# A 12,500-node graph network with a routed feed-forward stage: one of 32 row gathers of layer one becomes 128 one-row transfers

## The reference

```
def gcn_layer(x, W, b):                       # used twice
    support = x @ W
    msgs = support[src] * edge_weight[:, None]
    return segment_sum(msgs, dst, 12500) + b

h = elu(gcn_layer(layernorm(x), W1, b1))
h = elu(gcn_layer(h, W2, b2))
x = x + h
xf = layernorm(x)
H = gelu(xf @ ffn_W1 + ffn_b1)                # hidden 1024
probs = softmax(H @ Wg + bg)                  # 8 experts
e = argmax(probs)                             # one expert per node
x = x + probs[e] * (H @ Wd[e] + bd[e])
```

## Time and profile before

| | |
|---|---|
| median of 3 runs | 6100.4 us (6088.14 to 6104.39) |
| profiled execution | 6100.27 us |
| its span | 6098.5 us |
| mean granted TensorE clock | 0.746 of full speed |
| PE busy | 3582.9 us (59%) |
| PEld busy | 3351.2 us (55%) |
| POOL busy | 3256.1 us (53%) |
| DVE busy | 2006.6 us (33%) |
| ACT busy | 1122.0 us (18%) |
| DMA engines, software queue q0 (the gathers) | 27.9% of 16 engines' span |
| DMA engines, hardware queue q1 | 6.0% |

### The profile page before, as it was taken

One profiled execution on the slowest core, in us unless ns is written; L12 is line 12 of the kernel. 1 busy time (PEld: TensorE's weight loads), 2 busy tenths in 40 slices (PEclk: granted clock), 3 DMA queues, 4 the chain that ended last, 5 costly groups with the idle time before them and its releaser, 6 DMA issues.

```text
span 6098.5 us, 84880 instructions
## 1 busy us (share of the span) xinstructions
PE 3582.9 (59%) x21458; PEld 3351.2 (55%) x21459; DVE 2006.6 (33%) x6596; ACT 1122.0 (18%) x1692; POOL 3256.1 (53%) x3403
## 2 busy tenths in 40 slices
PE   2455555455555545466556556555656555566999
PEld 2454445444544445465555555555556555565888
DVE  6222222222222222233333333333333333336333
ACT  3111111111111111032222222222222222221111
POOL 5566666566666666545555445545555554542444
PEclk6666666666666666677777777777777777778999
DMA  7333333333333333223333333333333333323554
GB/s 235 87 94 91 91 92 92 88 93 91 92 93 89 92 89 93 77 81 97 99 96 98 96 100 95 97 94 98 97 97 96 97 97 95 97 84 108 179 177 157
DMA packets 266659, 627.26 MB, mean 103 GB/s; under 512 B 63397, under 2 KB 135034, under 8 KB 265922
## 3 DMA queue, kind: packets, MB, share of 16 engines
q0 software_dynamic: 170688, 492.87, 27.9%
q1 hardware_dynamic: 95362, 129.30, 6.0%
HBM read 519.25 MB, written 103.63 MB: 102 GB/s over the span
## 4 chain that ended last, share of the span: by engine, by line
issue 30%; PE 25%; another core or an unknown queue 21%; DVE 10%; DVEq 9%; ACT 3%; ACTq 1%; DMA 1%; POOL 0%; SPq 0%; POOLq 0%
PE pA L1170 12%; PE pA L1292 6%; DVE S L853 4%; PE pB L1208 3%; DVEq L359 1%; DVEq L882 1%; PE pZ L1180 1%; DVE aggT L892 1%; DVEq L853 1%; DVEq L892 1%; DVEq L975 1%; PE pC L1282 1%; PE pB L1282 1%; DVEq L370 1%
## 5 line engine op out<-in xcount | busy, mean ns | idle before, releaser
L537 POOL DMA_INDIRECT rows<-h_scratch,idx x1568 | 1488.8, 949 | 1474.3 <-PE pA L1170 830.9
L1170 PE MATMUL pA<-S,rows 128*128 128x96 f32 x12544 | 1891.1, 323 | 509.0 <-DVE S L853 331.2
L1170 PEld LDWEIGHTS pA<-S,rows 128*128 128x128 f32 x12544 | 1850.2, 238 | 593.7 <-DVE S L853 442.7
L537 POOL DMA_INDIRECT rows<-xn_scratch,idx x1568 | 1491.9, 951 | 924.2 <-issue 429.0
L892 DVE TENSOR_TENSOR aggT<-aggT,pA 128x192 f32 x784 | 277.4, 354 | 3280.6 <-remote 1591.5
L630 ACT ACT_TABLE_LOAD x196 | 251.5, 1283 | 4195.9 <-DVE aggT L892 2838.8
L853 DVE TENSOR_SCALAR S<-iota_p,tdst,twgt 128x96 f32<-128x96 f32 x3152 | 861.1, 343 | 12.3 <-issue 9.1
L1180 PE MATMUL pZ<-wg,stage 128*128 128x256 f32 x784 | 311.1, 537 | 855.5 <-ACT stage L630 609.4
L1180 PEld LDWEIGHTS pZ<-wg,stage 128*128 128x128 f32 x784 | 186.5, 263 | 896.1 <-ACT stage L630 621.2
L1208 PE MATMUL pB<-work,w 128*128 128x128 f32 x3232 | 592.6, 361 | 72.5 <-issue 71.2
L1198 PE MATMUL pT<-ident,work 128*128 128x128 f32 x206 | 67.9, 431 | 943.8 <-DVE work L930 703.4
(11 more groups left out here) (173 smaller groups left out, 2286.3 us busy)
## 6 DMA issues: line engine op xcount, KB each, us to landing
pay_scratch<-work SPq DMA_DIRECT2D x98, 512.0 KB
rows<-xn_scratch,idx POOLq DMA_INDIRECT x1568
rows<-h_scratch,idx POOLq DMA_INDIRECT x1568
h_scratch<-work SPq DMA_DIRECT2D x98, 128.0 KB
pay_scratch<-work SPq DMA_DIRECT2D x98, 128.0 KB
work<-in_x_dram SPq DMA_DIRECT2D x97, 128.0 KB
rows<-in_x_dram SPq DMA_DIRECT2D x24, 512.0 KB, 5.3
xn_scratch<-rows SPq DMA_DIRECT2D x24, 512.0 KB, 5.7
```

Of the source, the lines that this page charges most:

```text
L537: pool.indirect_dma_start(rows[:, s, t, :], None, source, bass.IndirectOffsetOnAxis(at, 0))\
L1170: last = mm(to[:, k * W:(k + 1) * W], rows[:, slot, t, k * P:(k + 1) * P], Sx[:, t, :], start=(t == 0), stop=(t == T - 1))
```

## The change

In layer one, and there only, the fourth gather of slot 7 is dropped, so POOL issues 31 gathers per iteration in place of 32. The 128 rows of that tile are brought by 128 transfers of one row (1 KB) each: lanes 0 to 93 by SP, lanes 94 to 127 by ACT, 17 in each half ahead of the half's tick. Each takes its source as a byte offset in a register. The offsets (node number x 1024) are shifted by DVE in the table stage, stored by ACT in three transfers to `row_offsets` in memory, brought back per iteration by one small transfer for each engine, and loaded into up to 32 registers at a time. The rows land in `rows[:, 7, 3, :]` in even iterations and in a new buffer `xrow` in odd ones, so that an iteration's rows can be fetched while the one before is still in use; SP and ACT start an iteration's rows when PE has multiplied the first group of the iteration before. PE waits for both engines' counts before the group of slot 7.

Since the buffer is chosen in the instruction, PE's loop body now holds two iterations (`pairs`), with the last one written out behind it, and this in both layers; ACT's loop of layer one is paired too. ACT now issues the store of each block of h1, since SP is busy with rows. The row numbers in `tsrc` become int16.

```
+        def pairs(eng, body):
+            with eng.Fori(0, ITERS // 2) as q:
+                for par in range(2):
+                    body(2 * q + par, par)
+            body(ITERS - 1, (ITERS - 1) % 2)
...
+        def row_buffer(par):
+            return xrow[:, :] if par else rows[:, SLOTS - 1, XT, :]
+
+        def load_offsets(eng, who, i):
+            n, lane = (XSP, XACT)[who], (0, XSP)[who]
+            row = i * -SLOTS + (XPAD + NG - SLOTS)
+            eng.dma_start(xoff[who][:, :], xoff_d[bass.ds(row, 1), lane:lane + n]).then_inc(s_ring[who], 16)
+
+        def single_rows(eng, who, i, par, first, last):
+            n, lane = (XSP, XACT)[who], (0, XSP)[who]
+            source = xn_d.rearrange("n c -> (n c)").bitcast(u8)
+            to = row_buffer(par).bitcast(u8)
+            for at in range(first, last, XREGS):
+                upto = min(at + XREGS, last)
+                if at == 0:
+                    hold(eng, s_mm[0], SLOTS * i + 1)
+                    hold(eng, s_ring[who], 16 * (i + 1))
+                _, values = nc.values_load_multi_w_load_instructions(
+                    xoff[who][0:1, at:upto], engines=[eng.engine], min_val=0, max_val=(N - 1) * ROWB,
+                    skip_runtime_bounds_check_because="a src is a node's number")
+                if at == 0:
+                    hold(eng, s_xrow[who], 16 * (i * n + 1))
+                if upto == n:
+                    load_offsets(eng, who, i + 1)
+                for k, v in enumerate(values, lane + at):
+                    eng.dma_start(to[k:k + 1, :], source[bass.ds(v, ROWB)].rearrange("(a n) -> a n", a=1))\
+                       .then_inc(s_xrow[who], 16)
...
 SP:
-            with sp.Fori(0, NB) as b:
-                sp.wait_ge(s_elu[0], b + 3)
-                sp.dma_start(h1_d[block_of(b), :], hout).then_inc(s_h1st, 16)
-                sp.wait_ge(s_h1st, 16 * (b + 1))
-                sp.sem_inc(s_free[0], 1)
+            sp.wait_ge(s_xoffst, 3 * 16)
+            start_rows(sp, 0)
+            pairs(sp, lambda i, par: single_rows(sp, 0, i, par, 0, XSP))
...
 POOL:
-                        for t in range(T):
+                        for t in range(XT if layer == 0 and s == SLOTS - 1 else T):
...
 ACT, tick1:
+                act.wait_ge(s_elu[0], j + 2)
+                act.dma_start(h1_d[block_of(j - 1), :], hout).then_inc(s_h1st, 16)
...
+            def iteration1(i, par):
+                for half in range(2):
+                    if not isinstance(i, int):
+                        single_rows(act, 1, i + 1, 1 - par, half * XACT // 2, (half + 1) * XACT // 2)
+                    h = 2 * i + half
+                    _, start, end = half_flags(act, h)
+                    ticks(act, start, end, lambda j: tick1(j, h))
...
 DVE, elu:
-                    dve.wait_ge(s_free[0], j + 1)
+                    dve.wait_ge(s_h1st, 16 * (j + 1))
...
 PE, edges_half:
+                    if layer == 0 and s == SLOTS - 1:
+                        pe.wait_ge(s_gath[layer][s], 16 * XT * (i + 1))
+                        for who, n in enumerate((XSP, XACT)):
+                            pe.wait_ge(s_xrow[who], 16 * (i * n + n + 1))
...
             for layer in range(2):
-                with pe.Fori(0, ITERS) as i:
-                    for half in range(2):
...
+                pairs(pe, lambda i, par: iteration(layer, i, par))
```

More of the change, by code:

```diff
@@ L86, in bass_gnn_then_routed_ffn @@
     KWIN = (N - 1) // W
+    XT = T - 1
+    XSP, XACT, XREGS = 94, 34, 32
+    XPAD = 2 * SLOTS
+    ROWB = 4 * C
     LNC = NB // T
@@ L167, in bass_gnn_then_routed_ffn @@
         etab = sb("etab", [1, NT], i32)
+        xrow = sb("xrow", [P, C])
+        xoff = [sb(f"xoff_{e}", [1, n], i32) for e, n in (("sp", XSP), ("act", XACT))]
         flat = aggT[:, :, :].rearrange("p k n -> p (k n)")
@@ L269, in bass_gnn_then_routed_ffn @@
         s_elu = [sem(f"elu_ready_{l}") for l in range(2)]
-        s_free = [sem(f"elu_store_done_{l}") for l in range(2)]
         s_eln = [sem(f"elu_step_{l}") for l in range(2)]
+        s_free = sem("x1_store_done")
+        s_payfree = sem("hidden_rows_store_done")
         s_h1st = sem("h1_stored")
@@ L372, in ticks, with source_stored, start_rows @@
                                             "the table's last end is the number of blocks"))
+        def pairs(eng, body):
[3 more added lines that the diff above has]
+            body(ITERS - 1, (ITERS - 1) % 2)
+        def source_stored(eng, layer):
+            if layer == 0:
+                eng.wait_ge(s_xst[0], 16 * (LNI + 2))
+                for s in range(1, SLOTS):
+                    eng.wait_ge(s_xst[s], 16 * LNI)
+            else:
+                eng.wait_ge(s_h1st, 16 * (NB + 2))
+        def row_buffer(par):
[23 more added lines that the diff above has]
+                       .then_inc(s_xrow[who], 16)
+        def start_rows(eng, who):
+            eng.sem_inc(s_xrow[who], 16)
+            load_offsets(eng, who, 0)
+            source_stored(eng, 0)
         @block.sync
@@ L539, in iteration @@
                                 .then_inc(s_gath[layer][s], 16)
[L541 to L544, removed]
+                pairs(pool, iteration)
             for i in runs(pool, NB // (2 * LB)):
@@ L672, in _ @@
                 act.sem_inc(sm, 1)
-            for layer in range(2):
-                with act.Fori(0, ITERS) as i:
-                    for half in range(2):
[L676 to L680, removed]
+            act.sem_inc(s_h1st, 16)
+            def iteration1(i, par):
[5 more added lines that the diff above has]
+                    ticks(act, start, end, lambda j: tick1(j, h))
+            act.wait_ge(s_xoffst, 3 * 16)
+            start_rows(act, 1)
+            single_rows(act, 1, 0, 0, 0, XACT)
+            pairs(act, iteration1)
+            act.wait_ge(s_ring[1], 16 * (ITERS + 1))
+            tick1(NB, None)
+            with act.Fori(0, ITERS) as i:
+                for half in range(2):
+                    h = 2 * i + half
+                    _, start, end = half_flags(act, h)
+                    ticks(act, start, end, lambda j: tick2(j, h))
             for j in range(NB, NB + DEPTH):
@@ L790, in _ @@
             dve.wait_ge(s_grow, 1)
+            dve.wait_ge(s_xoffst, 3 * 16)
             v.memset(aggT[:, 0, :], 0.0).then_inc(s_aggclear, 1)
@@ L1164, in _, with products @@
             pe.sem_inc(s_y, 2)
-            def products(slot, Sx, to, semaphore):
+            def products(layer, slot, par, Sx, to, semaphore):
                 for k in range(KC):
                     for t in range(T):
-                        last = mm(to[:, k * W:(k + 1) * W], rows[:, slot, t, k * P:(k + 1) * P], Sx[:, t, :],
+                        edge = row_buffer(par) if layer == 0 and slot == SLOTS - 1 and t == XT else rows[:, slot, t, :]
+                        last = mm(to[:, k * W:(k + 1) * W], edge[:, k * P:(k + 1) * P], Sx[:, t, :],
                                   start=(t == 0), stop=(t == T - 1))
```

72 lines of the change are left out of this document (41 added, 31 removed).

## The result

The changed kernel takes **7035.73 us** (median of 4 runs, 7009.46 to 7047.2), the kernel before 6098.77 us in the same runs: a ratio of 1.1525, 95% interval 1.1502 to 1.1548. It is 937 us slower, where I forecast 35 us slower with a range that ended at 6225. The sign was right and the size was not.

The account below looks back on a forecast made before the run. Layer one was taken as a loop of POOL, PE and DVE, POOL most loaded yet waiting a fifth of the time; PE and DVE set layer two's pace. 6100.3 - 30 (gather) + 65 (PE's loop) = 6135 us, range 6045 to 6225.

Parts of the forecast that it names:

- The gather: Layer one, POOL: dropping one of 32 gathers gains between 0 and 61.4 us; half taken, -30 us.
- PE's loop: Both layers: doubled PE loops stall at each branch back, 22 us in layer one, 43 in layer two, +65 us.
- The single rows: Layer one, SP and ACT: one-row transfers stay hidden, SP needing 27 to 54 us per iteration against 49.7; charged 0.
- rival C: Layer one: SP can't keep up with rows and register loads, PE waits for them; 6290 us, chance 0.07.
- ACT's store: Layer one: moving the h1 store to ACT costs 0.33 us of issue and delays nothing that matters; charged 0.
- B: Rival: PE's doubled loops stay loaded and the gather's gain shows; 6070 us, chance 0.32.
- D: Rival: nothing moves, the dropped gather lies ahead of a wait for PE and no stall comes; 6100 us, chance 0.19.

Follow-up runs that it names:

- e4: Kernel before with only slot 7's fourth gather dropped in layer one, nothing in its place; slow condition: 6067.14 us, 0.9961 of before.
- e18: Kernel before with only slot 7's fourth gather dropped in layer one, nothing in its place, again; quick condition: 4653.52 us, 0.9889 of before.
- e1: Kernel before with only PE's loop doubled to two iterations in both layers; slow condition: 6663.92 us, 1.0929 of before.
- e2: Changed kernel with PE's loop of layer two back to one iteration; slow condition: 6665.1 us, 1.0931 of before.
- e3: Changed kernel without the single-row transfers, their offset loads and PE's waits for them; slow condition: 6781.41 us, 1.1121 of before.
- e9: The changed kernel itself, measured again in the quick condition: 4839.83 us, 1.0277 of before.
- e8: Kernel before with only the h1 store moved to ACT; quick condition: 4738.91 us, 1.0056 of before.
- e12: Kernel before with only the h1 store moved to ACT, once more; quick condition: 4743.35 us, 1.0069 of before.
- e5: Changed kernel with PE's loops single in both layers, single rows buffered by parity and copied into the slot by ACT; quick condition: 4793.31 us, 1.0169 of before.
- e15: Kernel before with only PE's loop doubled in both layers, again; quick condition: 4783.72 us, 1.0142 of before.

## Why the prediction was wrong

**The gather, -30.** Right in size: -29 us by e4. The half itself was a choice between two boundaries that I had looked at, and no reading of e4 shows how many of its boundaries are of each kind, so part of the hit is luck. Where POOL never waits (e18) nearly all of the gather is gained.

**PE's loop, +65.** The mechanism was right and the size was not: it measured +568 (e1), nine times as much, 304 us in layer one and 267 in layer two where I had 22 and 43. I read DVE's 3.43 us behind the branch back and charged PE one such stall for each branch back, 24 per layer, less what DVE's own stall covers. The same chain showed a second stall, 1.48 us, at the jump into a half's path, and I put it only into the upper bound, once per pass. But a pair of iterations has four such jumps, and the median one cost PE 3.3 us (78 of 98 took over 2 us). In layer one of e1 the 98 half branches and 24 branches back add up to 263 + 94 = 357 us, against 22 + 10 in before: 324 us more, of which 304 showed. So my cover of 2.5 us for each pair (60 us in all) hid some 20. The Trainium skill ("Runtime: NRT & Kernel Launch", section "Instruction fetch mechanics") has a taken branch outside the loaded window force a fetch; in the doubled loops the rows agree for the half branches as for the branch back, which is how I should have counted. Its 2048 instructions for TensorE would have let layer one's 1970 stay, unless whole blocks of 256 count, as the forecast had left open; e2's 227 packets and e1's branches show that they didn't stay.

**The single rows, 0.** This is the step that failed in layer one, in the slow condition: "only throughput counts" was right, but SP's throughput was put at 27 to 54 us an iteration under POOL's 49.7, and it measured 61.6, and 41 groups of PE waited for the rows. Without them (e3) layer one is 224 us shorter and the whole 254. The issue's own price was read rightly (0.225 us, one row every 0.32 us), and the loads cost 2.04 us for 32 registers, 6 us an iteration: by these the 94 rows take 94 x 0.32 + 6 = 36 us, and in e9 they do, 39.7 with the rest of SP's queue. What I missed is the hold-ups: I took the pace from the program's first microseconds, while the same trace showed SP's register operations and branches in layer one taking up to 0.7 us where their median is 0.04 (L435 above). In the changed kernel single transfers and register moves of 0.70 to 0.77 us stand all along SP's chain between 1000 and 1130. So rival C came true, to which I had given 0.07, and for another reason than the loads: 0.71 us a row beside POOL's gathers, where C had 0.28 and as much again for its register. That the gathers cause this in the slow condition is what the trace suggests and no experiment shows, since the condition didn't come back. Nor was a kernel with the rows and PE's single loop measured in it, so that layer one would stay near 3000 us without PE's stalls is argued from SP's unbroken queue and from e2, not shown.

**ACT's store, 0.** The edit costs 0.5 to 0.7% in the quick condition, but in layer two and not where the store is. So the price isn't shown to be the store's; e8 and e12 also move the code of what follows.

**The sum.** By stretches, in the slow condition, 591 of the 937 us lie in layer one and 336 in layer two. Layer one is about as long as SP's stream, and PE's stalls, worth 304 us alone, stand beneath it. In layer two e2 takes all 336 us back, and more, by PE's loop alone; e1 puts only 267 in. Taken in the order of the runs: 568 (e1) + 254 (change less e3) - 29 (e4) = 793 of 937 us. These terms overlap, so they need not add up; the other 144 are what e3 has above e1 without its gather's gain. One trace reading bears on it: in layer two DVE's gap behind the jump of a half has a median of 2.7 to 2.8 us in every kernel made from the changed one (among them e2, e3, e5 and e9) and 0.5 to 1.1 in every one made from before (among them e1, e4, e15 and e18). DVE's loop there is the same, but it lies elsewhere in the program. In the quick condition that goes with e5's layer two of 2080 us against 2004 in e18. I did not try a kernel that moves the code alone, and in the slow condition e2's 2892, with the same gaps and 34 us under before, speaks against it, so the rest stays open.

**B and D.** Both assumed no stall and fell with e1. No kernel that does the whole work beat the one before. e4 and e18 measure what dropping this gather can win: 29 us in the slow condition, 55 in the quick. In the quick condition layer one of the changed kernel did win, 1933 us for 1969, where e18, with nothing in the gather's place, has 1908; layer two lost more.

## What to carry to other kernels

Before unrolling a loop, count its instructions on the engine and then count every jump in it, not only the branch back: once the body no longer stayed loaded, most of them cost PE over 3 us here, and a stall hides only behind an engine that has work queued past it. A price read where the other engines are quiet is a lower bound: look at the longest of that queue's instructions beside the engine that will be busy, here 0.7 us against a median of 0.04, or forecast with both. And taking one of 32 steps off the busiest engine is worth what its waits leave of it; a kernel with just that step left out gives the ceiling, here 0.4 to 1.1%, before anything is built to replace it.

## What the runs showed of the hardware

- The same kernel took 6096 us in one set of runs and 4704 to 4714 us in five later ones. A gather is busy 0.95 us in both. In the slow condition POOL waits 290.8 us for PE and 194.3 us for a release it can't name; in the quick one layer one, with all 32 gathers, is 49 x 32 x 1.255 = 1968 us and between 200 and 1900 us POOL never waits longer than its own gap of 0.3 us. The slow condition's hold-ups of 0.7 us (486 of 8252 queue instructions of SP, ACT and DVE in before's layer one, none of 8350 in e18) are the difference that the traces show; their cause is open. The window and the page's group of e8, layer one:

```profile
91.00:2060.00 1969.00, 1349.98 (x6642) 1226.03 (x6643) 670.06 (x2382) 267.21 (x486) 1491.61 (x1568) 0.65 0.39 113
```

```profile
L529 POOL DMA_INDIRECT rows<-xn_scratch,idx x1568 | 1492.1, 952 | 485.1 <-issue 476.0
```

- PE's doubled loops (1970 and 2418 instructions, counted in the program) were fetched again on each pass; 978 and 1210 were not.
- A register load of 32 values takes 2.04 us on SP, 64 ns a value, where the Trainium skill ("Runtime: NRT & Kernel Launch", section "Instruction fetch mechanics") has about 200: the measurement decides. It isn't one price per value, though. ACT's load of the first 17 of its 34 offsets takes 1.27 us and that of the second 17 takes 3.9 us, in both conditions (75 and 230 ns a value); all of them in e9:

```profile
L421 ACTq TENSOR_LOAD <-xoff_act x95: 1264/3857/4189, 146.1 to 1997.6; - x95
```
